# Two feed-forward phases of a macaron block: Hadamard folding by sums on VectorE, norms and low-rank projections placed among another tile's products

## The reference

```python
x = x + 0.5 * ffn(layernorm(x))
x = x + attn(layernorm(x))
x = x + 0.5 * ffn(layernorm(x))

def ffn(x):                                       # INTER = 1024, SCALE = 64
    x = fwht(x * SU_ug) / SCALE                   # Walsh-Hadamard transform over 256
    x_up   = x @ W_up.T   * (Wscale_ug[:INTER] * SCALE)
    x_gate = x @ W_gate.T * (Wscale_ug[INTER:] * SCALE)
    x = silu(x_gate) * x_up
    x = fwht(x * SU_dp) / SCALE                   # over 1024
    return x @ W_down.T * (Wscale_dp * SCALE)
```

## Time and profile before

| | us |
|---|---|
| median of three runs | 5188.24 (5179.7 to 5207.36) |
| the profiled execution, its own time | 5182.31 |
| its span in the trace | 5180.5 |
| first feed-forward phase (until SyncE issues the delta rule's first DMA) | 338.16 |
| delta rule | 4620.24 |
| second feed-forward phase (from its first DMA) | 222.10 |

### The profile page before, as it was taken

The page is one execution under the profiler, slowest core; times in us unless marked ns, Lnnn a source line. Parts: engine busy times, 40 slices in busy tenths (PEclk is TensorE's granted clock), DMA queues, the critical chain, the costliest instruction groups (busy, mean ns, idle before and its releaser), DMA issues.

```text
span 5180.5 us, 151658 instructions
## 1 busy us (share of the span) xinstructions
PE 4622.2 (89%) x63328; PEld 3207.9 (62%) x63328; DVE 4129.0 (80%) x7248; ACT 3469.5 (67%) x6767; POOL 3213.2 (62%) x5316
## 2 busy tenths in 40 slices
PE   7867999999999999999999999999999999998878
PEld 4434666666666666666666666666666666666645
DVE  1238999889999888999888898888999898888321
ACT  1246777777777777777777777777777777776421
POOL 0006777777777777777677777677777777777300
PEclk9888999999999999999999999999999999999679
DMA  2020000000010000000100000000000000000010
GB/s 75 31 77 22 25 24 24 24 14 24 26 32 29 28 24 14 23 25 24 33 30 20 22 25 24 24 25 19 23 28 24 24 24 24 19 19 9 2 45 17
DMA packets 49325, 135.54 MB, mean 26 GB/s; under 512 B 7040, under 2 KB 28160, under 8 KB 47872
## 3 DMA queue, kind: packets, MB, share of 16 engines
q1 hardware_dynamic: 48640, 125.84, 7.0%
HBM read 111.66 MB, written 14.16 MB: 24 GB/s over the span
## 4 chain that ended last, share of the span: by engine, by line
PE 56%; DVE 26%; ACT 11%; issue 6%; POOL 1%; DMA 1%; SPq 0%; DVEq 0%; ACTq 0%
PE bank L639 46%; DVE acc L1297 8%; DVE X L1294 6%; PE bank L289 5%; PE bank L296 2%; DVE sp_t L1294 2%; ACT o L954 2%; ACT L1204 2%; ACT Us L953 1%; DVE Pd L1402 1%; DVE Zc L1481 1%; DVE o L1297 1%; DVE Rs L1297 1%; PE bank L710 1%; ACT L1234 1%
## 5 line engine op out<-in xcount | busy, mean ns | idle before, releaser
L1297 DVE SCALAR_TENSOR_TENSOR acc<-bank,vc,acc 128x510 f32<-128x510 f32 (+2 forms) x1728 | 1271.9, 739 | 141.7 <-ACT acc L953 113.7
L1718 POOL TENSOR_TENSOR LZ<-LZ,LT 128x120 f32<-128x120 f32 (+26 forms) x1984 | 948.1, 478 | 155.5
L1715 POOL TENSOR_TENSOR LT<-LA,LZ 128x120 f32<-128x120 f32 (+26 forms) x1984 | 919.5, 463 | 145.9
L1294 DVE TENSOR_TENSOR X<-KQ,Fl 128x640 f32<-128x640 f32 x1024 | 1000.6, 993 | 1.5 <-ACT Fl L954 1.5
L1688 POOL COPY X<-KQ 128x640 f32<-128x640 f32 x256 | 247.1, 965 | 1025.7 <-ACT F L954 375.7
L639 PE MATMUL bank<-X 128*32 128x60 f32 (+1 forms) x32768 | 658.1, 206 | 132.5 <-DVE Pd L1402 87.5
L639 PEld LDWEIGHTS bank<-X 128*32 128x32 f32 x32768 | 531.1, 113 | 367.6 <-issue 210.4
L639 PE MATMUL bank<-xnTm,WK 128*128 128x512 f32 x1280 | 659.6, 641 | 47.3 <-DVE acc L1297 33.7
L953 ACT ACTIVATE Us<-bank 128x128 f32<-128x128 f32 x1024 | 280.0, 275 | 629.4 <-PE bank L639 623.5
L639 PE MATMUL bank<-Rs,Ztf 128*128 128x128 f32 x2048 | 477.5, 320 | 68.8 <-DVE Rs L1297 47.7
L1667 POOL TENSOR_TENSOR kdec<-KQ,Fe 128x512 f32<-128x512 f32 x256 | 339.1, 1325 | 298.1 <-PE bank L710 298.1
(11 more groups left out here) (138 smaller groups left out, 9453.2 us busy)
## 6 DMA issues: line engine op xcount, KB each, us to landing
WK<-in_wkq SPq DMA_DIRECT2D x64, 704.0 KB, 6.0
WV<-in_wv SPq DMA_DIRECT2D x64, 576.0 KB, 3.9
WO<-in_wo SPq DMA_DIRECT2D x64, 128.0 KB, 2.0
xt<-in_x SPq DMA_DIRECT2D x4, 512.0 KB, 5.4
wut<-in_wu SPq DMA_DIRECT2D x1, 2048.0 KB, 10.3
wuh_d<-wuh SPq DMA_DIRECT2D x1, 2048.0 KB, 6.3
x_d<-x SPq DMA_DIRECT2D x4, 512.0 KB, 3.1
xnT_d<-xT SPq DMA_DIRECT2D x4, 512.0 KB, 2.7
```

The costliest lines, as they stand in the source:

```text
L1294: return e.tensor_tensor(o, a, b, op)
L1297: return e.scalar_tensor_tensor(out=o, in0=a, scalar=sc, in1=b, op0=op0, op1=op1)
L1715: e.tensor_tensor(tmp, LA[:, j + 1:32, 8 * (j % R) + j // R].unsqueeze(2).broadcast_to([P, rr, cc]), LZ[:, j, 0:cc].unsqueeze(1).broadcast ...
L1718: e.tensor_tensor(LZ[:, j + 1:32, 0:cc], LZ[:, j + 1:32, 0:cc], tmp, SUB).then_inc(g_row, 1)
```

## The change

The Hadamard fold now works in two steps. The sign matrix of 2 (up, gate) is done by one sum and one difference on VectorE for each 512 columns (`fly_up`, eight instructions of 128x512); the one of 8 (down) by three rounds of one sum and one difference each (`fly_down`, six instructions of 128x1024). TensorE then does one product with `had` for each result: 8 matmuls of 512 columns in place of 16, and 8 of 256 columns in place of 64. `nhad` is gone. The raw weights land in `wuh` and `wdh`; `wut` and `wdt` hold the sums. The up and gate weights come as two DMAs, and `d_w` is split in three (`d_wu`, `d_wd`, `d_low`); the constants `cs`, which were the first DMA, now stand seventh.

Within the tiles the norm of tile n+1 is computed between the steps k of tile n (`spread` after k = 3, `inverse` and `normal` after k = 4), and its transposes stand between gate/up and down of tile n. The norm of tile n's result comes on VectorE right after the additions of down, as before; its transposes and the products with `f1w`, `g1w` and `bw` (`low(n)`) stand between k = 3 and k = 4 of tile n+1, and the last tile's at the end. ScalarE no longer waits for up before it takes gate. The second phase waits for `wuh` before gate/up and for `wdh` before down, no longer for both before its first transposes.

```diff
             f.uses = []
             if first:
-                f.uses += [("wu", a, n, "act") for a in range(2) for n in range(4)]
+                f.uses += [("wu", a, n, "act") for n in range(4) for a in range(2)]
                 f.uses += [("wd", a, 0, "vec") for a in range(8)]
+            f.uses += [("ln", 0, hf, "act") for hf in range(2)]
             for n in range(NT):
-                f.uses += [("ln", n, hf, "act") for hf in range(2)]
                 for k in range(8):
+                    if k == 4 and first and n:
+                        f.uses += low_uses(n - 1)
                     f.uses += [("gate", n, k, "act"), ("up", n, k, "vec")]
+                if n + 1 < NT:
+                    f.uses += [("ln", n + 1, hf, "act") for hf in range(2)]
                 f.uses += [("down", n, j, "vec") for j in range(4)]
-                if first:
-                    f.uses += [("ln2", n, hf, "act") for hf in range(2)]
-                    f.uses += [("f", n, 0, "act"), ("g", n, 0, "act")]
-                    f.uses += [("beta", n, j, "act") for j in range(4)]
+            if first:
+                f.uses += low_uses(NT - 1)
...
+        def low_uses(n):
+            return ([("ln2", n, hf, "act") for hf in range(2)] + [("f", n, 0, "act"), ("g", n, 0, "act")]
+                    + [("beta", n, j, "act") for j in range(4)])
...
         def ffn_sync(e, f):
             w = Stream(e)
-            e.dma_start(f.fv[:, :], fvec).then_inc(f.d_fv, 16)
-            e.dma_start(f.xt[:, 0], f.src[0]).then_inc(f.d_x[0], 16)
             if f.first:
-                e.dma_start(f.wut[:, :, :], wu).then_inc(f.d_w, 16)
-                e.dma_start(f.wdt[:, :, :], wd).then_inc(f.d_w, 16)
-                e.dma_start(f.wsb[:, :], wsd).then_inc(f.d_w, 16)
-                e.dma_start(f.hd[:, :, :], cst[:, C_HAD:C_END].rearrange("p (a c) -> p a c", a=2)).then_inc(f.d_w, 16)
-                e.dma_start(f.f1w[:, :, :], wf1).then_inc(f.d_w, 16)
-                e.dma_start(f.g1w[:, :, :], wg1).then_inc(f.d_w, 16)
-                e.dma_start(f.bw[:, :, :], wb).then_inc(f.d_w, 16)
-                e.dma_start(f.b1[:, :], bg1).then_inc(f.d_w, 16)
+                for h in range(2):
+                    e.dma_start(f.wuh[:, :, INTER * h:INTER * h + INTER], wu[:, :, INTER * h:INTER * h + INTER]).then_inc(f.d_wu[h], 16)
+                    if h == 0:
+                        e.dma_start(f.hd[:, :], cst[:, C_HAD:C_END]).then_inc(f.d_wu[0], 16)
+                e.dma_start(f.fv[:, :], fvec).then_inc(f.d_fv, 16)
+                e.dma_start(f.wdh[:, :, :], wd).then_inc(f.d_wd, 16)
+                e.dma_start(f.xt[:, 0], f.src[0]).then_inc(f.d_x[0], 16)
+                e.dma_start(cs[:, :], cst[:, 0:C_HAD]).then_inc(d_cst, 16)
+                e.dma_start(f.wsb[:, :], wsd).then_inc(f.d_wd, 16)
+                e.dma_start(f.f1w[:, :, :], wf1).then_inc(f.d_low, 16)
+                e.dma_start(f.g1w[:, :, :], wg1).then_inc(f.d_low, 16)
+                e.dma_start(f.bw[:, :, :], wb).then_inc(f.d_low, 16)
+                e.dma_start(f.b1[:, :], bg1).then_inc(f.d_low, 16)
             else:
-                e.dma_start(f.wuh[:, :, :], wuh_d).then_inc(f.d_w, 16)
-                e.dma_start(f.wdh[:, :, :], wdh_d).then_inc(f.d_w, 16)
+                e.dma_start(f.fv[:, :], fvec).then_inc(f.d_fv, 16)
...
+            def store_low(n):
+                w.wait_ge(*f.emptied[f.place["beta", n, 3]])
+                e.dma_start(xnT_d[n], f.xT2[:, n % 2]).then_inc(f.d_p[n % 2], 16)
+                e.dma_start(fg_d[n], f.fg[:, n % 2]).then_inc(f.d_p[n % 2], 16)
+                e.dma_start(by_tile(beta_d)[n], f.bt[:, n % 2]).then_inc(f.d_p[n % 2], 16)
...
+            def fold_up(n):
+                w.wait_ge(f.d_wu[0], 32)
+                w.wait_ge(f.s_fly, 2 * n + 2)
+                for a in range(2):
+                    o = bank_for("wu", a, n)
+                    mm(o[:, :], f.hd[:, :], f.wut[:, a, 512 * n:512 * n + 512], True, True).then_inc(f.s_mm, 1)
+
+            def fold_down():
+                w.wait_ge(f.s_fly, 14)
+                for a in range(8):
+                    o = bank_for("wd", a, 0)
+                    mm(o[:, 0:D], f.hd[:, :], f.wdt[:, a, :], True, True).then_inc(f.s_mm, 1)
...
-            if f.first:
-                had, nhad = f.hd[:, 0, :], f.hd[:, 1, :]
-                w.wait_ge(f.d_w, 128)
-                for a in range(2):
-                    for n in range(4):
-                        o = bank_for("wu", a, n)
-                        for b in range(2):
-                            ins = e.matmul(o[:, :], nhad if a & b else had, f.wut[:, b, 512 * n:512 * n + 512],
-                                           start=b == 0, stop=b == 1, skip_group_check=True)
-                        ins.then_inc(f.s_mm, 1)
-                for a in range(8):
-                    o = bank_for("wd", a, 0)
-                    for b in range(8):
-                        ins = e.matmul(o[:, 0:D], nhad if bin(a & b).count("1") % 2 else had, f.wdt[:, b, :],
-                                       start=b == 0, stop=b == 7, skip_group_check=True)
+            def gate_up(n, k):
+                w.wait_ge(*f.emptied[f.place["ln", n, 1]])
+                if f.first:
+                    w.wait_ge(*f.emptied[f.place["wu", 1, 3]])
+                else:
+                    w.wait_ge(f.d_wu[0], 16)
+                for what, off in (("gate", INTER), ("up", 0)):
+                    o = bank_for(what, n, k)
+                    for hf in range(2):
...
+            def down(n):
                 w.wait_ge(*f.emptied[f.place["up", n, 7]])
+                if f.first:
+                    w.wait_ge(*f.emptied[f.place["wd", 7, 0]])
+                else:
+                    w.wait_ge(f.d_wd, 16)
...
+            def low(n):
+                turn("ln2", n, 1)
+                w.wait_ge(f.d_low, 64)
                 w.wait_ge(*f.emptied[f.place["ln2", n, 1]])
...
+            if f.first:
+                for n in range(4):
+                    fold_up(n)
+                fold_down()
+            turn("ln", 0, 0)
+            for n in range(NT):
+                for k in range(4):
+                    gate_up(n, k)
+                if f.first and n:
+                    low(n - 1)
+                for k in range(4, 8):
+                    gate_up(n, k)
+                if n + 1 < NT:
+                    turn("ln", n + 1, 0)
+                down(n)
+            if f.first:
+                low(NT - 1)
 
...
+            def deviation(n, count):
+                w.wait_ge(d_cst, 16)
+                w.wait_ge(f.s_ln[count], nth(n, 4, 1))
+                e.activation(f.sd[:, 0:4], f.mv[:, :, 1], ACT.Sqrt, bias=eps_c).then_inc(f.s_sd[count], 1)
+
+            def turned(n):
                 if n:
                     w.wait_ge(f.s_mm, ffn_done(f, "up", n - 1, 7))
...
+            def gate(n, k):
+                w.wait_ge(f.s_s1, 2)
+                if n or k > 1:
+                    w.wait_ge(*f.emptied[f.place[("up", n, k - 2) if k > 1 else ("up", n - 1, k + 6)]])
+                e.activation(f.gs[:, k % 2, :], full("gate", n, k)[:, :], ACT.Silu,
+                             scale=f.s1[:, 8 + k:9 + k]).then_inc(f.s_act, 1)
...
+            if f.first:
+                for n in range(4):
+                    fold_up(n)
+            deviation(0, 0)
+            turned(0)
+            for n in range(NT):
+                if f.first and n:
+                    deviation(n - 1, 1)
+                for k in range(4):
+                    gate(n, k)
+                if f.first and n:
+                    low(n - 1)
+                if n + 1 < NT:
+                    deviation(n + 1, 0)
+                for k in range(4, 8):
+                    gate(n, k)
+                if n + 1 < NT:
+                    turned(n + 1)
+            if f.first:
+                deviation(NT - 1, 1)
+                low(NT - 1)
+
...
+            def fly_up(n):
+                w.wait_ge(f.d_wu[n // 2], 32 if n < 2 else 16)
+                c = slice(512 * n, 512 * n + 512)
+                e.tensor_tensor(f.wut[:, 0, c], f.wuh[:, 0, c], f.wuh[:, 1, c], ADD).then_inc(f.s_fly, 1)
+                e.tensor_tensor(f.wut[:, 1, c], f.wuh[:, 0, c], f.wuh[:, 1, c], SUB).then_inc(f.s_fly, 1)
+
+            def fly_down(i, src, dst):
+                w.wait_ge(f.d_wd, 32)
+                w.wait_ge(f.s_fly, 8 + 2 * i if i else 0)
+                s4 = src[:, :, :].rearrange("p (m two b) d -> p m two (b d)", two=2, b=1 << i)
+                d4 = dst[:, :, :].rearrange("p (m two b) d -> p m two (b d)", two=2, b=1 << i)
+                e.tensor_tensor(d4[:, :, 0], s4[:, :, 0], s4[:, :, 1], ADD).then_inc(f.s_fly, 1)
+                e.tensor_tensor(d4[:, :, 1], s4[:, :, 0], s4[:, :, 1], SUB).then_inc(f.s_fly, 1)
...
+            def norm_after(n):
+                x1n = f.x1[:, n % 2]
+                w.wait_ge(*f.emptied[f.place["down", n, 3]])
```

(41 more changed lines are left out.)

167 lines of the change are left out of this document (56 added, 111 removed).

## The result

The changed kernel takes 5047.8 us in the median (5041.7 to 5059.3, four runs), the kernel before 5185.7 beside it; the ratio is 0.973 with a 95% interval of 0.970 to 0.976. That is 138 us less. The forecast was 5055, the range 5033 to 5085.

A forecast was written before the change was run, and what follows sets the result against it. TensorE's own chain (work, idle stretches, lower-clock stretches) was taken to bound the feed-forward phases. Gains of 96.7 and 32.8 us, together 129.5, took the profiled 5182.3 to 5052.8, moved up to 5055; range 5033 to 5085.

The forecast's parts named there:

- start of the first gate/up: First phase, TensorE: with the new fold and load order gate/up starts at 29.7 us in place of 67.15, 37.5 less.
- idle before the middle transposes, and the tail: First phase: TensorE's idle time for norms goes, hidden under the next tile's gate/up, 27.2 us; shorter last norm, 1.4.
- gate/up at full clock, first phase: First phase: with no stop above 1 us before it, gate/up falls from 119.5 to 109.8 us, 9.7 less.
- transposes: First phase: six middle sets take 1.07 us each instead of 11.8 together, 5.3 less.
- products with f1w and g1w: First phase, low-rank products: 6.2 us per tile against four matmuls at 0.86; 7.5 us less in all.
- stops before gate/up, before down: First phase, TensorE's idle time: 2.1 us goes before gate/up in three of four tiles, 6.0 before down.
- first phase: First feed-forward phase: the start and tile terms together make it 96.7 us shorter.
- second phase: Second feed-forward phase: earlier transposes, full-speed gate/up, hidden norms and shorter stops together make it 32.8 us shorter.
- The clock: TensorE, feed-forward phases: stops of about 4 us also cost lower-clock time behind them; gate/up terms 9.7 and 7.5 us.
- The rival that the clock falls all the same: Feed-forward phases: gate/up, low-rank products and transposes stay as slow as before; 33 us less gain, 5088 us; chance 0.08.
- The tail: First phase, last tile: its norm waits 4.4 us instead of 5.74, the root's table being loaded earlier; 1.4 us less.
- The cover: Within tiles: added VectorE and ScalarE work costs nothing, since TensorE needs the bank only four steps or 13.7 us later.

The follow-up runs named there:

- second profile: The changed kernel run once more, unchanged, for a second profile: 5047.1 us in the median, ratio 0.974 to the kernel before.
- Two experiments that open stops of 4.2 to 4.3 us again: Changed kernel with the low-rank piece back behind its own tile's down: ratio 0.980; with the next tile's norm behind down in the second phase alone: 0.982.
- the early start: Changed kernel with scales, first tile and constants loaded earlier, first norm before down's sums, down's fold inside the first tile's gate/up: 5051.1 us, ratio 0.975.

## Why the prediction was right

By its own steps, forecast against measured:

| term | forecast | measured |
|---|---|---|
| start of the first gate/up | 29.7 (37.5 less) | 31.2, 31.0 (36.0 less) |
| idle before the middle transposes, and the tail | 27.2 + 1.4 | 27.2 + 1.4 (of the waits for norms one of 4.33 is left) |
| gate/up at full clock, first phase | 9.7 | 119.5 - 111.3 = 8.2; 6.5 in the second profile |
| transposes | 5.3 | 14.8 - 9.2 = 5.6 |
| products with f1w and g1w | 7.5 | 24.9 - 17.5 = 7.4 |
| stops before gate/up, before down | 2.1, 6.0 | 2.1, 6.1 |
| first phase | 96.7 | 95.5, 93.4 |
| second phase | 32.8 | 34.2, 34.1 |

The measured terms of the first phase add up to 94.0; 1.5 us of the 95.5 are in none of them. Gate/up did reach the full clock after the start: from its start to that of the next group it took 27.57 us in the first tile and 13.74 and 13.79 for the halves, so 27.5 per tile where 27.4 was forecast. It is now cut into seven stretches, not four, and each adds the time by which neighbouring records overlap.

**The clock** was the main mechanism, and it held: of the 129.8 us, 8.2 and 7.5 are gate/up at full speed, 5.6 the transposes and 7.4 the low-rank products of the first phase. Two experiments that open stops of 4.2 to 4.3 us again bring 0.50 back. The rival that the clock falls all the same is refuted for the transposes (24 times over) and for the stops of 0.7 to 0.8 us in the middle of the tiles. At the start of the first gate/up it did fall in two of seven profiles, at a cost of 1.7 us.

**The start** came within 1.5 us, in part by luck: it had three misses, and one stood in for part of the other two. The prediction let the up products end early and charged the down products at the lower clock, so that they would be what the transposes wait for. They ran at full speed, behind a stop of 1.25 us, because VectorE's sums waited until 11.0 us for a small load that the prediction had not looked at. Its own bound without that charge was a gate/up at 28.4, and gate/up came at 31.2, because the other two misses go the other way. `wsb` landed at 16.7, not 14.6: the load did have its gaps, as the core's DMAs moved 102 to 283 GB/s in each microsecond from 2 to 6 us, where they had moved 225 to 357 before; why, no run shows. And the norm took 5.1 us, not 3.8, as the root's table was loaded in the open. So the transposes waited for VectorE's norm and scalings, not for the products. In the experiment with the scales first, the products at the lower clock are the wait, as forecast.

**The tail** went as forecast: in the last tile ScalarE loaded the root's table at 206.59, far ahead of the variance, and the wait was 4.33 instead of 5.74.

**The cover** for VectorE's and ScalarE's new work held: there is no stop in the middle of a tile but the copy of `xT2` (0.74 to 0.83 us). The banks and the norm's place on VectorE were not moved in an experiment, so how much room is left is not shown.

**The size.** The two feed-forward phases give 129.8 us, and 127.6 by the second profile. The medians give 138 and, in the second comparison, 132. The profiled execution of the changed kernel is the slowest of its four (5059.3), so the two profiled executions differ by 123.0 only. The feed-forward phases repeat within about 2 us, the delta rule within 26, so these differences are of the size of the delta rule's scatter. The forecast moved from 5052.8 up to 5055 on the ground of one execution below its median; the measured median is 5047.8. The prediction's sign that it would be wrong if the delta rule's length changed by more than 10 us was set too tight: the second profile of the changed kernel is 16.5 us shorter there than the first of the kernel before, with the same text of the delta rule.

## What to carry to other kernels

A stop costs what stands behind it too: here three waits of 4.2 to 4.3 us for a norm cost 13 us and 8 to 10 more through the clock, and work put between the products gave both back. A norm, a root or a small projection should stand among another tile's products, as long as the banks leave the engine that feeds them some steps of room. When an early start is tuned, look in each engine's queue for the small thing that others stand behind, and at what an earlier engine then does. A load of 13 KB decided when TensorE began, but to have it earlier gained nothing, since the next wait (for `wsb`, behind the large transfers) stayed and the stop before it grew. A root behind eight scalings took the gain of the early start (243.5 us for the first phase, 236.5 with the root behind four).

## What the runs showed of the hardware

- The load of the scales (13 KB) took 1.6 to 1.8 us from issue to landing when it was the first of the kernel (three runs), and 8.3 us as the fourth, behind two transfers of 1024 KB and one of 64.
- In seven profiles with the same start TensorE stopped for 1.17 to 2.28 us before the down products, for 1.7 before the transposes and for 0.74 before gate/up. The down products took 3.72 us in all seven. Gate/up began at the lower clock in the two with a first stop of 1.57 and 1.59 us, and in none of the five others. A stop of 5.95 us before the down products brought 0.50 in their first 4 us.
- Float32 transposes held the clock: 192 in a row, 20.9 us at 1.00, and 13.98 us for down behind them.
- ScalarE loaded the table of the root in the open at 25.68 us, after the variance was there, but ahead of its wait at 60.55 us (the root itself came at 76.19). At the first place the program still waits for two semaphores, at the second for one. That the number of waits decides this was not tried.
- In the fold's first stretch the window shows a granted clock of 1.00 (12.59 to 23.93 us), while the matmuls there took 800 ns in the mean against 593 in gate/up. Their weight loads follow one another at 0.86 us until 17.85 and at 0.43 from 18.65 on, as at the lower and the full clock. At the very start the records tell more than the clock column.
